# Moving the product with Wlin from GpSimd to VectorE, the copy of the values to ScalarE, and spreading the gathers

## The reference

```python
embed_x = emb_table[X + offsets[None, :]]            # 2048 x 39 x 64
att = embed_x
for i in range(3):                                   # _mhsa, 2 heads of 32
    scores = einsum('bihd,bjhd->bhij', q, k)         # 39 x 39 per sample and head
    out = einsum('bhij,bjhd->bihd', softmax(scores), v) + att @ WR[i]
    att = relu(out)
att_output = relu(att.reshape(B, 39 * 64) @ Wlin)    # one number per sample
h = relu(embed_x.reshape(B, 39 * 64) @ W1 + b1)      # 512
h = relu(h @ W2 + b2)                                # 256
return sigmoid(att_output + relu(h @ W3 + b3))
```

## Time and profile before

| | |
|---|---|
| median of 3 runs | 2331.08 us (2326.01 to 2338.38) |
| the profiled execution | 2338.26 us |
| its span | 2336.0 us, 105692 instructions |
| PE busy | 2074.0 us (89%) |
| DVE busy | 1783.2 us (76%) |
| ACT busy | 1225.8 us (52%) |
| POOL busy | 1263.2 us (54%) |

### The profile page before, as it was taken

How to read it: one execution, slowest core, us unless ns; L and a number is a source line. 1 busy time by engine, 2 the same in 40 slices (tenths; PEclk the granted TensorE clock), 3 DMA queues, 4 the chain that set the end, 5 groups by cost and what they waited for, 6 DMA issues and landing times. The chain is left out here.

```text
span 2336.0 us, 105692 instructions
## 1 busy us (share of the span) xinstructions
PE 2074.0 (89%) x44640; PEld 1687.1 (72%) x44640; DVE 1783.2 (76%) x3943; ACT 1225.8 (52%) x3397; POOL 1263.2 (54%) x1838
## 2 busy tenths in 40 slices
PE   1798998988989899898989989989898998989998
PEld 0577776867767777676777767778687776767887
DVE  2677786867868787786787868778687787878997
ACT  0455554645645455564555545556464555545665
POOL 6445555555555655556455555655656555565503
PEclk9999999989999999998999989999999999999998
DMA  4110011101101011010110101011010110101000
GB/s 137 26 26 24 24 28 24 28 22 24 28 23 28 23 28 25 23 29 21 27 26 25 28 22 28 23 25 29 22 30 23 27 25 24 29 21 27 23 20 15
DMA packets 67580, 64.76 MB, mean 28 GB/s; under 512 B 23768, under 2 KB 54504, under 8 KB 67112
## 3 DMA queue, kind: packets, MB, share of 16 engines
q1 hardware_dynamic: 47144, 37.52, 5.3%
q0 software_dynamic: 19968, 20.49, 4.6%
HBM read 27.24 MB, written 0.01 MB: 12 GB/s over the span
## 5 line engine op out<-in xcount | busy, mean ns | idle before, releaser
L314 POOL DMA_INDIRECT emb<-L_rec_emb_table,idx_t x624 | 640.1, 1026 | 532.5 <-PE Ob L472 350.2
L642 DVE TENSOR_REDUCE den<-pe_sb 103x16 f32<-103x624 f32 x384 | 308.5, 803 | 293.5 <-ACT pe_sb L567 277.6
L553 ACT ACTIVATE xs<-Ob 128x312 f32<-128x312 f32 x384 | 166.2, 433 | 672.1 <-PE Ob L472 661.8
L630 DVE TENSOR_REDUCE mx<-SV 103x8 f32<-103x312 f32 x768 | 365.1, 475 | 170.4 <-PE SV L455 156.4
L455 PE MATMUL SV<-yv,xs 64*39 64x142 f32 x12288 | 481.7, 296 | 10.7 <-ACT yv L560 8.0
L578 ACT COPY pt<-X 103x312 f32<-103x312 f32 x768 | 288.8, 423 | 259.3 <-PE X L441 201.3
L455 PEld LDWEIGHTS SV<-yv,xs 64*39 64x39 f32 x12288 | 359.3, 117 | 60.5 <-issue 10.4
L472 PEld LDWEIGHTS Ob<-pt,v_sb 39*32 39x32 f32 x12288 | 285.8, 109 | 152.7 <-issue 151.2
L472 PE MATMUL Ob<-pt,v_sb 39*32 39x39 f32 x12288 | 350.0, 201 | 51.5 <-ACT pt L578 25.9
L636 DVE TENSOR_TENSOR sd<-SV,mx 103x312 f32<-103x312 f32 x768 | 364.2, 474 | 0.0
L472 PE MATMUL Ob<-pt,v_x 39*32 39x39 f32 x12288 | 338.2, 202 | 25.7 <-issue 24.5
(11 more groups left out here) (74 smaller groups left out, 2670.5 us busy)
## 6 DMA issues: line engine op xcount, KB each, us to landing
v_x<-v_sb SPq DMA_DIRECT2D x768, 39.0 KB
emb<-L_rec_emb_table,idx_t POOLq DMA_INDIRECT x624
w<-L_rec_W SPq DMA_DIRECT2D x1, 4864.0 KB
w<-L_rec_W SPq DMA_DIRECT2D x1, 512.0 KB
idx_in<-r_X SPq DMA_DIRECT2D x1, 312.0 KB, 3.7
b_b<-L_rec_b SPq DMA_DIRECT2D x1, 256.0 KB
w<-L_rec_W SPq DMA_DIRECT2D x1, 128.0 KB
b_b<-L_rec_b SPq DMA_DIRECT2D x1, 128.0 KB
```

The lines of the kernel that those rows point to most:

```text
L314: nc.gpsimd.indirect_dma_start(out=emb[:, n % ER, f % 2 * D:(f % 2 + 1) * D], out_offset=None, in_=table, in_offset=bass.IndirectOffsetOnA ...
L630: nc.vector.tensor_reduce(mx[:, gs, :], sv_scores[:, gs], AX.X, ALU.max).then_inc(mx_ready, 1)
L642: nc.vector.tensor_reduce(den[:], pe_sb[:], AX.X, ALU.add).then_inc(den_ready, 1)
```

## The change

GpSimd keeps gathers and shuffles alone. `lin` is gone. For the units of the last layer there is no relu on ScalarE any more: VectorE reads Ob directly, takes the maximum with 0 and multiplies with Wlin in one instruction (`weighted`), and adds up 39 numbers per sample and row in one reduction (`summed`). The copy of the values goes from VectorE to ScalarE, as one copy of 512 columns behind an exp that is now one instruction of 624 columns; v_ready therefore comes from ScalarE, and TensorE waits for it before the next scores in place of the two subtractions. VectorE now does both maxima, then both subtractions. ScalarE makes x_hi ahead of the copies yv. The gathers start two steps earlier in a tile, nearly all steps issue two, and four of the five steps with a shuffle issue none; chunks may be transposed from step -3 on, and most of them three steps after their gathers.

```diff
-    NEXT = 19
-    FIELDS_AT = [2, 1, 2, 1, 1, 2, 2, 2, 2, 1, 1, 1, 2, 2, 2, 2, 2, 1, 2, 2, 2, 1, 2, 1]
-    FIRST_FIELDS_AT = [9] + FIELDS_AT[5:6] * 8 + FIELDS_AT[9:18]
-    SHUFFLE_AT = {9: 0, 10: 1, 11: 2, 17: 3, 21: 4}
-    LIN_AT = {20: 0, 22: 1, 23: 2, 0: 3, 1: 4, 2: 5, 3: 6, 4: 7}
-    LIN_FROM = 20
+    NEXT = 17
+    FIELDS_AT = [2, 2, 2, 2, 2, 2, 2, 2, 1, 2, 0, 2, 0, 2, 2, 0, 2, 2, 2, 0, 2, 2, 2, 2]
+    FIRST_FIELDS_AT = [10] + 9 * [2] + [1, 2, 1, 2, 2, 1, 2]
+    SHUFFLE_AT = {8: 0, 10: 1, 12: 2, 15: 3, 19: 4}
-    CHUNK_STEPS = chunk_steps(GATHERED, -LAG, 2 - LAG)
+    CHUNK_STEPS = chunk_steps(GATHERED, -LAG, -3)
...
 # TensorE
-                    at_least(pe, sd_ready, 2 * (u - 1) + j + 1)
+                    if j == 0:
+                        at_least(pe, v_ready, u)
...
-                at_least(pe, x_new, min(u, TOTAL))
+                if 0 < u <= TOTAL:
+                    if layer_of(u - 1) == L - 1:
+                        pe.wait_ge(lin_mult, last_outputs(u - 1))
+                    else:
+                        pe.wait_ge(x_new, outputs(u - 1))
...
 # ScalarE
-                if 0 <= u < TOTAL:
+                if 0 <= u < TOTAL and layer_of(u) < L - 1:
                     act.wait_ge(o_ps, u + 1)
                     nc.scalar.activation(xs[:, layer_of(u) + 1, layer_cols(u)], Ob[:, 0:C], ACTF.Relu).then_inc(x_new, 1)
                 if chunk_at(s - 1):
+                    at_least(act, o_ps, s - PV_AT)
                     evacuate_embedding(*chunk_at(s - 1))
+                if s + LEAD < TOTAL:
+                    split_high(s + LEAD)
...
                     at_least(act, pn_ready, u)
-                    for j in range(2):
-                        act.wait_ge(sd_ready, 2 * u + j + 1)
-                        nc.scalar.activation(half(pe_sb, j), half(sd, j), ACTF.Exp).then_inc(e_ready, 1)
-                if s + LEAD < TOTAL:
-                    split_high(s + LEAD)
+                    act.wait_ge(sd_ready, 2 * u + 2)
+                    nc.scalar.activation(pe_sb[:], sd[:], ACTF.Exp).then_inc(e_ready, 1)
+                    at_least(act, o_ps, u - VS + 1)
+                    nc.scalar.copy(v_sb[:, u % VS, :, :, :], sv_values).then_inc(v_ready, 1)
...
 # VectorE
+            def weighted(u):
+                dve.wait_ge(o_ps, u + 1)
+                if chunk_at(u + PV_AT):
+                    dve.wait_ge(embT_ready, chunk_count(*chunk_at(u + PV_AT)))
+                at_least(dve, lin_sum, last_outputs(u) - 1)
+                nc.vector.scalar_tensor_tensor(out=prod[:].rearrange("q (p f) -> q p f", f=F),
+                                               in0=Ob[:, 0:C].rearrange("q (p f) -> q p f", f=F), scalar=0.0,
+                                               in1=wl[:, None, :].to_broadcast([128, UP, F]),
+                                               op0=ALU.max, op1=ALU.mult).then_inc(lin_mult, 1)
+            def summed(u):
+                dve.wait_ge(lin_mult, last_outputs(u))
+                at = u // NU * NP + u % UL * UP
+                nc.vector.tensor_reduce(red[:, at:at + UP], prod[:].rearrange("q (p f) -> q p f", f=F),
+                                        AX.X, ALU.add).then_inc(lin_sum, 1)
...
                 for j in range(2):
-                    gs = slice(j * (G // 2), (j + 1) * (G // 2))
                     dve.wait_ge(sv_ps, 2 * s + j + 1)
-                    nc.vector.tensor_reduce(mx[:, gs, :], sv_scores[:, gs], AX.X, ALU.max).then_inc(mx_ready, 1)
-                    copied = nc.vector.tensor_copy(v_sb[:, s % VS, :, gs, :], sv_values[:, :, gs])
-                    if j == 1:
-                        copied.then_inc(v_ready, 1)
+                    nc.vector.tensor_reduce(mx[:, regions(j), :], sv_scores[:, regions(j)], AX.X, ALU.max).then_inc(mx_ready, 1)
+                at_least(dve, e_ready, s)
+                for j in range(2):
+                    gs = regions(j)
                     dve.wait_ge(mx_ready, 2 * s + j + 1)
-                    at_least(dve, e_ready, 2 * (s - 1) + j + 1)
                     nc.vector.tensor_tensor(sd[:, gs], ...).then_inc(sd_ready, 1)
+                u = s - PV_AT
+                if u >= 0 and layer_of(u) == L - 1:
+                    weighted(u)
                 if s + LEAD < TOTAL:
                     split_low(s + LEAD)
+                if u >= 0 and layer_of(u) == L - 1:
+                    summed(u)
-                dve.wait_ge(e_ready, 2 * s + 2)
+                dve.wait_ge(e_ready, s + 1)
```

More of the change, by code:

```diff
@@ L132, in autoint @@
         embT = sb("embT", [128, 2, FC, TB])
-        xs = sb("xs", [128, L + 1, XC])
+        xs = sb("xs", [128, L, XC])
+        prod = sb("prod", [128, C])
         x_hi = sb("x_hi", [128, XS, C], F32R)
@@ L189, in autoint @@
         h2w_ready = sem("h2w_ready")
-        lin_step = sem("lin_step")
-        red_done = sem("red_done")
-        red_last = sem("red_last")
+        lin_mult = sem("lin_mult")
+        lin_sum = sem("lin_sum")
         dchain = sem("dchain")
@@ L221, in autoint, with regions @@
         block = ctx.enter_context(nc.Block())
-        def half(tile, j):
-            return tile[:, j * (G // 2):(j + 1) * (G // 2)].rearrange("q g h f -> q (g h f)")
+        def regions(j):
+            return slice(j * (G // 2), (j + 1) * (G // 2))
         def landed(eng, t, f):
@@ L239, in tile_step, with outputs, last_outputs @@
             return s // NU, s % NU
+        def outputs(u):
+            return u // NU * (NU - UL) + min(u % NU + 1, NU - UL)
+        def last_outputs(u):
+            return u // NU * UL + max(u % NU + 1 - (NU - UL), 0)
         def layer_cols(u):
@@ L327, in shuffle_for @@
                 pool.wait_ge(shuffled, t * NB * 4 + k * 4 + 4)
[L329 to L347, removed]
             pool.wait_ge(idx_ready, 1)
@@ L358, in _ @@
                 shuffles = ts in SHUFFLE_AT and t + 1 < TILES
-                lin_tile = t if ts >= LIN_FROM else t - 1
-                lins = ts in LIN_AT and lin_tile >= 0
-                if shuffles or lins:
+                if shuffles:
                     for back in range(min(4, s + 1)):
@@ L364, in _ @@
                             landed(pool, fields_at(s - back)[0], f)
-                if shuffles:
                     shuffle_for(t + 1, SHUFFLE_AT[ts])
[L367 to L370, removed]
         @block.tensor
@@ L504, in _ @@
                     attended(u)
-            pe.wait_ge(red_done, TILES * UL - 1)
-            pe.wait_ge(red_last, 1)
+            pe.wait_ge(lin_sum, TILES * UL)
             for t in range(TILES):
@@ L536, in split_high @@
                 else:
-                    act.wait_ge(x_new, u - UL + 1)
+                    act.wait_ge(x_new, outputs(u - UL))
                 at_least(act, o_ps, u - XS + 1)
@@ L548, in _ @@
                 u = s - NEW_AT
-                if 0 <= u < TOTAL:
+                if 0 <= u < TOTAL and layer_of(u) < L - 1:
                     act.wait_ge(o_ps, u + 1)
-                    if layer_of(u) == L - 1:
-                        at_least(act, red_done, (u // NU - 1) * UL + u % UL + 1)
                     nc.scalar.activation(xs[:, layer_of(u) + 1, layer_cols(u)], Ob[:, 0:C], ACTF.Relu).then_inc(x_new, 1)
                 if chunk_at(s - 1):
+                    at_least(act, o_ps, s - PV_AT)
                     evacuate_embedding(*chunk_at(s - 1))
+                if s + LEAD < TOTAL:
+                    split_high(s + LEAD)
                 if s < TOTAL:
@@ L622, in _ @@
                 split_low(u)
+            def weighted(u):
[12 more added lines that the diff above has]
+                                        AX.X, ALU.add).then_inc(lin_sum, 1)
             for s in range(TOTAL):
                 t, ts = tile_step(s)
-                at_least(dve, o_ps, s - VS + 1)
                 for j in range(2):
-                    gs = slice(j * (G // 2), (j + 1) * (G // 2))
                     dve.wait_ge(sv_ps, 2 * s + j + 1)
-                    nc.vector.tensor_reduce(mx[:, gs, :], sv_scores[:, gs], AX.X, ALU.max).then_inc(mx_ready, 1)
-                    copied = nc.vector.tensor_copy(v_sb[:, s % VS, :, gs, :], sv_values[:, :, gs])
-                    if j == 1:
-                        copied.then_inc(v_ready, 1)
+                    nc.vector.tensor_reduce(mx[:, regions(j), :], sv_scores[:, regions(j)], AX.X, ALU.max).then_inc(mx_ready, 1)
+                at_least(dve, e_ready, s)
+                for j in range(2):
+                    gs = regions(j)
                     dve.wait_ge(mx_ready, 2 * s + j + 1)
-                    at_least(dve, e_ready, 2 * (s - 1) + j + 1)
                     nc.vector.tensor_tensor(sd[:, gs], sv_scores[:, gs],
@@ L660, in _ @@
                     nc.vector.tensor_reduce(dnn[:, t:t + 1], h2w[:], AX.X, ALU.add)
[L661 to L665, removed]
+            for u in range(TOTAL - PV_AT, TOTAL):
+                weighted(u)
+                summed(u)
             dve.wait_ge(fin_pe, 1)
```

## The result

The changed kernel takes 2072.5 us (2067.6 to 2074.0, 4 runs) against 2334.7 (2326.0 to 2343.3) beside it: a ratio of 0.887, 95% interval 0.884 to 0.891. The forecast was 2030, its range 1990 to 2180. In a later group of runs (the kernels of a group share a chip) the same two kernels took 2039.8 and 2289.0: 0.891 (0.887 to 0.895). The attended group is the 64 matmuls of the attended values of one step, and its length runs from the start of its first to the start of its last.

A forecast was written before the change was run, and what follows sets the result against it. TensorE bounds a clean step; late gathers behind GpSimd's `lin`, and the half clock behind them, cost the rest. Sixteen tiles of 120.6 us make 1930; start, first steps and end bring 2032, adjusted to 2030 us, range 1990 to 2180.

The forecast's parts named there:

- The waits go and the clock with them: TensorE's waits for gathers (102.2 us), issue (49.6) and pt (25.9) go to about nothing, and with them their half clock.
- the holes: Gaps of TensorE inside the attended values, 49.6 us of issue waits, put down to gathers issued beside those matmuls.
- median gather case: Attended group with a gather beside it: 1.5 us against 0.60, used to price a SyncE issue at 0.9 us a step.
- The clean step: TensorE's step when nothing is late: 5.00 us, PE busy throughout at full clock.
- The rival with SyncE's issues: SyncE's two DMA issues, moved past the attended values' start, starve TensorE: 0.9 us a step, 346 us, slower; chance 0.07.
- ScalarE's row: ScalarE's order in a step: x_hi, yv, exp 0.72 us, values copy 0.60, ended at 2.91, leaving 0.27 before the scores.
- The rule of the Trainium skill: VectorE empties its pipe between operations; without overlap an iteration takes 5.21 us, 27 us over 128 steps; forecast followed the trace.
- Step 23: Late maxima delay VectorE's weighted, whose Ob TensorE wants near 1.0: put at 5.6 us, longest step of a tile.
- the others keep 5.00: All 23 steps of a tile besides step 23 take 5.00 us each, so a tile takes 120.6.
- a sign of being right: Listed beforehand as showing the forecast right: a tile of 120 to 122 us.
- the tight place: Step 8's gather and four shuffles push step 9's gathers to 1.5 to 4.0, just ahead of the attended values at 4.3.
- they stay: Steps 0 to 2 of the run, 10.3 us over three clean ones, keep that excess; a tenth gather adds 1.3.

## Why the prediction was right, and where it was off

*The waits go and the clock with them: right.* 102.2, 49.6 and 25.9 us became 0, 6.7 and 0.3; the clock is 0.990, with 43 us at the half level, of which 34 in tile 0 (PEclk 0.89 over its 153 us). The cause that the forecast named, `lin` in GpSimd's queue, was shown by leaving `lin` out, with the old lists (0.880, one execution) and with the new (0.875).

*That the holes come from gathers beside the attended values: right as a mechanism, its size not.* The forecast took it from a coincidence, and in the experiment that put gathers there the groups grew. But the 49.6 us of holes belonged to that run; where they were missing, the same lateness showed as 159.4 us of waiting. That the saving came out nearly the same (ratios 0.887 and 0.891) fits the late queue being the cause of both. The forecast's "median gather case" of 1.5 us is 1.7 when counted over all 77 groups.

*The clean step.* A steady step was put at 5.00; where a relu runs it is 5.055. Ten to twelve such steps make 0.5 to 0.6 us a tile. The rival with SyncE's issues looked at the right place: the step loses 0.04 us there, not 0.9, and not by the issue itself.

*ScalarE's row: right.* 0.592 us forecast as 0.60, exp 0.741 as 0.72. It never holds TensorE in a steady step.

*VectorE: right.* The product costs 0.39 us from start to start. The rule of the Trainium skill ("VectorE: DVE Perf Modes", "The DRAIN you can't avoid"), read as one operation ending before the next begins, does not hold here: 0.47 long, 0.39 apart. The same section adds that an operation that is not held starts earlier, which the forecast left out, and the trace agrees with that. Step 23 came to 5.4, forecast 5.6; but it is not the longest of a tile, as the forecast had it: step 0 is.

*The step of the sum that failed: "the others keep 5.00".* A tile takes 122.6 us, not 120.6, and so lies outside the 120 to 122 that the forecast gave as a sign of being right. Step 0 has twice the dense matmuls, 5.87 us: 0.87 a tile, 14 us in all, and it was visible in the code and in the trace before. Step 18 is 5.33 (it was 5.3 before, too), steps 19 and 22 give 0.4 back. Step 9 is 5.42 at the median in the first trace, the tight place: 0.4; 5.17 in the second. By medians these, the steps with a relu and step 23 make 1.6 of the 2.0 us; the rest is single longer steps.

*The start was the other one.* Tile 0 was put at 136 us and took 153.0; in the later trace 125.2. ScalarE's 14.5 us of idle time in step 1, behind TensorE's wait of 11.2 us, was in the trace before as well, and the forecast took its cost over with "they stay" without asking what it was: steps 0 to 2 were put at 26.6 us and took 28.7. The rest of the excess lies in steps 3 to 23. The attended groups of steps 13, 17 and 21 had gathers beside them and took 2.2, 2.3 and 5.8 us; the forecast had 4 us for such. Why steps 10 and 18 took 8.8 and 8.5 us is open. I overestimated what follows the last step by some 4 us. Together: 17 from tile 0, 30 from the other tiles, less 4, near the 40 us that the span has over the forecast's 2032.

*What the forecast did not ask: which part earns it.* Counted in points of the ratio, leaving `lin` out is worth 12.0. With the old lists, having VectorE do it, and the copies on ScalarE, costs 2.7 (0.880 to 0.908); the new lists give 1.7 back (0.891). The lists are worth 4.1 points while `lin` is on GpSimd, and 0.5 without the product: what they earn depends on what else is late. Against the best that leaves the product out (0.875) the price of the product is 1.6 points, 37 us; of its 2.5 us a tile, 1.1 lie in steps 19, 22 and 23. x_hi ahead of yv and the new order of the maxima were not run apart.

## What to carry to other kernels

When an engine that only prepares work is 50% busy and still late, look at its queue, not at its share: take the long block out of the queue and the stalls behind it go (12 points here), while more lead time moved them and took back a third (4.1 points). Before counting steps as equal, list what each step of the period issues; one that has twice the matmuls is in the program text. An effect seen beside a stall in one trace should be priced from a second trace or from a run that puts it there.

## What was not expected of the hardware

An indirect gather issued on GpSimd beside 64 matmuls of 39 columns lengthens that group from 0.60 us to between 0.6 and 1.3 us in most traces, by where it starts, and to 1.7 at the median in the first. The 32 matmuls of the scores (142 columns) are not lengthened: in the changed kernel's first trace they take 0.90 us from the first start to the last at the median, with a gather beside them (102 steps, one over 1 us) and without (282). SyncE's DMA issues beside the attended group lengthen it not at all (348 steps, 0.60). The same kernels differ by up to 2% between groups of runs, and ratios by 0.4 points. Why the small matmuls are held up and these are not, and why by so much more in the first group of runs, no run here shows.
